# Transfers of 125 partitions as 112 and 13, and two first layer norms from one set of statistics

## The reference, cut to what matters

```
xn = LN(x)
x  = x + sage(xn, src, dst) + performer(LN(xn) * g1 + be1)   # kqv, exp features, gelu MLP
x  = x + attention(LN(x))                                    # router picks 1 of 3 weight sets, 8 heads, 1250 x 1250
xn = LN(x)
x  = x + gin(xn, adjacency) + slice_attention(xn)            # batch norms over the nodes
x  = x + moe(LN(x))    # 32 experts, each takes its top 39 of the 1250 tokens; 110 MB of weights
```

## Time and profile before

| | us |
|---|---|
| three runs | 1966.99, 1969.98, 1966.98 (median 1966.99) |
| profiled execution, whole | 1966.68 |
| its span in the trace | 1964.9 |

### The profile page before, as it was taken

The page is one execution under the profiler, slowest core; times in us unless marked ns, Lnnn a source line. Parts: engine busy times, 40 slices in busy tenths (PEclk is TensorE's granted clock), DMA queues, the critical chain, the costliest instruction groups (busy, mean ns, idle before and its releaser), DMA issues.

```text
span 1964.9 us, 19619 instructions
## 1 busy us (share of the span) xinstructions
PE 1617.7 (82%) x7674; PEld 1101.6 (56%) x7674; DVE 806.2 (41%) x1517; ACT 507.0 (26%) x734; POOL 391.3 (20%) x248
## 2 busy tenths in 40 slices
PE   1999969799998759888888886899889651999895
PEld 1546644366556548677777763555766541655452
DVE  5021160699204642577777755250344324111100
ACT  1210011021201132577777741100223110101000
POOL 3100030200301120344444424100220002222112
PEclk9999989899998879899999998999999855999997
DMA  4000100100110011100000012000200452799993
GB/s 171 0 0 1 41 4 0 59 1 1 82 46 1 6 65 66 27 14 14 14 14 14 22 37 120 0 22 0 86 1 0 206 206 95 285 403 400 408 418 126
DMA packets 23236, 170.74 MB, mean 87 GB/s; under 512 B 4259, under 2 KB 4805, under 8 KB 16886
## 3 DMA queue, kind: packets, MB, share of 16 engines
q1 hardware_dynamic: 19568, 164.44, 21.2%
q0 software_dynamic: 3584, 5.12, 1.2%
HBM read 153.06 MB, written 16.49 MB: 86 GB/s over the span
## 4 chain that ended last, share of the span: by engine, by line
PE 57%; DMA 16%; DVE 13%; ACT 6%; issue 5%; POOL 2%; another core or an unknown queue 1%; SPq 0%; DVEq 0%; POOLq 0%; ACTq 0%
PE psum L839 16%; DMA out_x<-arena,idx 12%; PE psum L849 9%; PE psum L866 6%; PE psum L978 6%; PE psum L1063 5%; PE psum L858 4%; PE psum L1051 3%; DVE arena_r L1458 3%; PE psum L1033 3%; DMA xf_dram<-arena 2%; DVE neg_max L1437 2%; ACT arena_r L762 1%; DVE ln_st L1217 1%; DVE arena L1225 1%
## 5 line engine op out<-in xcount | busy, mean ns | idle before, releaser
L839 PE MATMUL psum<-arena 125*128 125x512 f32 (+3 forms) x864 | 308.0, 518 | 14.2 <-DMA arena<-in_w_in 11.4
L839 PEld LDWEIGHTS psum<-arena 125*128 125x128 f32 (+1 forms) x864 | 164.5, 191 | 157.1 <-issue 143.3
L866 PE MATMUL psum<-arena 128*125 128x512 f32 (+3 forms) x464 | 163.0, 510 | 20.6 <-DVE arena L1565 9.0
L542 POOL TENSOR_SCALAR arena<-arena,row_inv 125x1250 f32<-125x1250 f32 x40 | 138.5, 3462 | 192.3 <-DVE row_inv L1445 192.3
L1198 PE MATMUL psum<-arena 128*39 128x512 f32 (+1 forms) x704 | 159.2, 609 | 13.0 <-DMA arena<-in_w_down 10.2
L1051 PE MATMUL psum<-ident,arena 125*125 125x125 f32 x800 | 125.8, 283 | 49.7 <-DVE arena_r L1458 48.4
L1458 DVE TENSOR_TENSOR arena_r<-psum,arena_r 125x500 fp32r<-125x500 f32 x200 | 131.9, 673 | 42.2 <-ACT arena_r L762 29.2
L1051 PEld LDWEIGHTS psum<-ident,arena 125*125 125x125 f32 x800 | 102.8, 188 | 63.0 <-DVE arena_r L1458 58.2
L762 ACT ACTIVATE arena_r<-psum 125x500 fp32r<-125x500 f32 x200 | 114.5, 587 | 87.9 <-PE psum L1051 87.8
L866 PEld LDWEIGHTS psum<-arena 128*125 128x125 f32 (+2 forms) x464 | 81.2, 191 | 99.1 <-issue 71.0
L978 PE MATMUL psum<-arena 125*125 125x512 bf16 (+1 forms) x588 | 120.1, 358 | 13.0 <-DVE arena L1349 11.5
(11 more groups left out here) (283 smaller groups left out, 2019.1 us busy)
## 6 DMA issues: line engine op xcount, KB each, us to landing
arena<-in_w_down SPq DMA_DIRECT2D x32, 2816.0 KB, 22.6
arena<-in_w_up SPq DMA_DIRECT2D x32, 682.5 KB, 19.7
a_spill<-arena SPq DMA_DIRECT2D x1, 6103.5 KB
arena<-a_spill SPq DMA_DIRECT2D x1, 6103.5 KB
bc<-k_dram SPq DMA_DIRECT2D x16, 312.5 KB, 4.3
gw<-in_gw SPq DMA_DIRECT2D x2, 2048.0 KB, 10.7
arena<-in_wkqv SPq DMA_DIRECT2D x1, 3072.0 KB, 16.5
arena<-in_x SPq DMA_DIRECT2D x10, 250.0 KB
```

Of the source, the lines that this page charges most:

```text
L542: pool.tensor_scalar(PR[i], PR[i], row_inv[:, i:i + 1], None, ALU.mult).then_inc(p_even, 1)
L839: ins = pe.matmul(o[0:w, lo:hi], lhs(c, m), rhs(c)[:, lo:hi], start=c == 0, stop=c == k - 1)
L866: ins = pe.matmul(o[0:p, 0:w], lhs(c, t), rhs(c, t), start=c == 0, stop=c == k - 1)
```

## The change

Every large transfer with X, XF or the adjacency on 125 partitions is made as two, of partitions 0 to 111 and 112 to 124 (`ROW_PARTS`), and what waits for it waits for 32 where it waited for 16. The x loads become three (one to a group) on SP with 112 partitions and three on ACT's queue with 13; `vec` moves to ACT's queue behind them, and `wkqv` ahead of the edge lists. The broadcast biases, also 125 partitions, stay as they are. Statistics are taken of x alone; the norm `mix1` comes first and straight from X, interleaved by group, and `xn` follows from the same statistics with a second column of powers, `xn_rs`.

```diff
+ROW_PARTS = (slice(0, 112), slice(112, TOK))
...
-LN_OUT = {n: TILES * i for i, n in enumerate(("xn", "mix1", "mix2", "ffn", "l1", "moe"))}
+LN_OUT = {n: TILES * i for i, n in enumerate(("mix1", "xn", "mix2", "ffn", "l1", "moe"))}
...
+            def store_rows(done, dst, src):
+                for rows_of in ROW_PARTS:
+                    sp.dma_start(dst[rows_of], src[rows_of]).then_inc(done, 16)
+
             x_v = a["x"].rearrange("(t p) d -> p t d", p=TOK)
-            for t in range(TILES):
-                load(f"x{t}", X[:, t], x_v[:, t])
-            load("vec", vec[:], a["vec"])
+            for g, (lo, hi) in enumerate(GROUPS):
+                load(f"x{g}", X[ROW_PARTS[0], lo:hi], x_v[ROW_PARTS[0], lo:hi])
+            load("wkqv", WKQV, a["wkqv"].rearrange("p (k n) -> p k n", k=C))
             load("edge_rows", edge_rows_i, a["dst_rows"])
             load("edges", edge_i[:, 0:EDGE_TILES], a["src_cols"])
             load("edges", edge_i[:, EDGE_TILES:2 * EDGE_TILES], a["dst_cols"])
-            load("wkqv", WKQV, a["wkqv"].rearrange("p (k n) -> p k n", k=C))
...
-            sp.dma_start(a_spill, part(6, 0, TILES * N, TOK)).then_inc(spilled, 16)
+            store_rows(spilled, a_spill, part(6, 0, TILES * N, TOK))
...
-            load("adj", part(6, 0, TILES * N, TOK), a_spill)
+            store_rows(loads["adj"], part(6, 0, TILES * N, TOK), a_spill)
...
-            sp.dma_start(out.rearrange("(t p) d -> p t d", p=TOK), X).then_inc(base_stored, 16)
+            store_rows(base_stored, out.rearrange("(t p) d -> p t d", p=TOK), X)
             sp.wait_ge(ln_out, LN_OUT["moe"] + TILES)
-            sp.dma_start(xf_dram.rearrange("(t p) d -> p t d", p=TOK), XF).then_inc(xf_stored, 16)
+            store_rows(xf_stored, xf_dram.rearrange("(t p) d -> p t d", p=TOK), XF)
...
-            for g in range(3):
-                rstd("xn", g)
+            for g, (lo, hi) in enumerate(GROUPS):
+                pool.wait_ge(ln_mv, LN_TILES["mix1", g])
+                pool.tensor_scalar(ln_rs[:, lo:hi], ln_mv_t[:, lo:hi, 1], 1.0 + LN_EPS, LN_EPS * LN_EPS,
+                                   ALU.mult, ALU.add).then_inc(ln_eps, 1)
+                pool.wait_ge(ln_eps, LN_NUMBER["mix1", g] + 1)
+                pool.tensor_tensor(ln_rs[:, lo:hi], ln_rs[:, lo:hi], minus_half[:, lo:hi], ALU.pow).then_inc(ln_rstd, 1)
+            done(pool.tensor_scalar(xn_rs[:], ln_mv_t[:, :, 1], LN_EPS, None, ALU.add))
+            pool.tensor_tensor(xn_rs[:], xn_rs[:], minus_half[:], ALU.pow).then_inc(xn_rstd, 1)
...
-            for g in range(3):
-                rstd("mix1", g)
-
             pool.wait_ge(loads["b2"], 16)
-            pool.wait_ge(ln_out, TILES)
+            pool.wait_ge(ln_out, 2 * TILES)
...
+            x_v = a["x"].rearrange("(t p) d -> p t d", p=TOK)
+            for g, (lo, hi) in enumerate(GROUPS):
+                act.dma_start(X[ROW_PARTS[1], lo:hi], x_v[ROW_PARTS[1], lo:hi]).then_inc(loads[f"x{g}"], 16)
+            act.dma_start(vec[:], a["vec"]).then_inc(loads["vec"], 16)
...
             for g in range(3):
-                stats("xn", g, X, lambda t: dve.wait_ge(loads[f"x{t}"], 16))
-            for g in range(3):
-                normalise("xn", g, X, XN)
-
-            for g in range(3):
-                stats("mix1", g, XN, lambda t: dve.wait_ge(ln_out, LN_OUT["xn"] + t + 1))
-            for g in range(3):
-                normalise("mix1", g, XN, XH1)
+                stats("mix1", g, X, lambda t: dve.wait_ge(loads[f"x{g}"], 32))
+                if g:
+                    normalise("mix1", g - 1, X, XH1)
+            normalise("mix1", 2, X, XH1)
+            dve.wait_ge(xn_rstd, 1)
+            for t in range(TILES):
+                dve.tensor_scalar(XN[:, t], X[:, t], ln_mv_t[:, t, 0:1], xn_rs[:, t:t + 1],
+                                  ALU.subtract, ALU.mult).then_inc(ln_out, 1)
```

More of the change, by code:

```diff
@@ L82 @@
 ADJ_COL = {x: COL["adj"] + n for n, x in enumerate(ADJ_ORDER)}
-LN_ORDER = [(n, g) for n in ("xn", "mix1", "mix2") for g in range(3)]
+LN_ORDER = [(n, g) for n in ("mix1", "mix2") for g in range(3)]
 LN_ORDER += [(n, g) for g in range(3) for n in ("sage", "ffn")]
@@ L128, in build @@
         ln_rs = sb("ln_rs", [TOK, TILES])
+        xn_rs = sb("xn_rs", [TOK, TILES])
         src_f = sb("src_f", [EDGE_TILE, EDGE_TILES])
@@ L286, in build @@
         ln_stats, ln_mv, ln_eps, ln_rstd, ln_out = [sem(n) for n in ("ln_stats", "ln_mv", "ln_eps", "ln_rstd", "ln_out")]
+        xn_rstd = sem("xn_rstd")
         dve_step, pool_step = sem("dve_step"), sem("pool_step")
@@ L318, in build @@
         loads = {n: sem("ld_" + n) for n in (
[1 row of a table removed]
+            "x0", "x1", "x2",
             "vec", "edges", "edge_rows", "wkqv", "wpt", "wo", "wm1", "wm2", "bv", "bo", "b2", "ws", "wn",
@@ L377, in _ @@
             sp.wait_ge(sel_ready, 1)
-            sp.wait_ge(spilled, 16)
+            sp.wait_ge(spilled, 32)
             sel = sp.value_load(sel_i[0:1, 0:1], min_val=0, max_val=2)
@@ L442, in _ @@
             sp.wait_ge(rows_free, ROW["gin_t"] + TILES)
-            sp.dma_start(out.rearrange("(t p) d -> p t d", p=TOK), X).then_inc(base_stored, 16)
+            store_rows(base_stored, out.rearrange("(t p) d -> p t d", p=TOK), X)
             sp.wait_ge(ln_out, LN_OUT["moe"] + TILES)
-            sp.dma_start(xf_dram.rearrange("(t p) d -> p t d", p=TOK), XF).then_inc(xf_stored, 16)
-            sp.wait_ge(base_stored, 16)
-            sp.wait_ge(xf_stored, 16)
+            store_rows(xf_stored, xf_dram.rearrange("(t p) d -> p t d", p=TOK), XF)
+            sp.wait_ge(base_stored, 32)
+            sp.wait_ge(xf_stored, 32)
             sp.wait_ge(rows_full, ROW["moe_t"] + 12)
@@ L602, in gather @@
                         in_offset=bass.IndirectOffsetOnAxis(ap=idx[:, e:e + 1], axis=0)).then_inc(gathered[b], 16)
-            pool.wait_ge(xf_stored, 16)
-            pool.wait_ge(base_stored, 16)
+            pool.wait_ge(xf_stored, 32)
+            pool.wait_ge(base_stored, 32)
             pool.wait_ge(rows_free, ROW["topk_t"] + 1)
@@ L695, in _ @@
             drain_cols("agg0", 4, lambda m: AGGT[:, m])
-            act.wait_ge(spilled, 16)
+            act.wait_ge(spilled, 32)
             act.wait_ge(loads["wn"], 16)
@@ L1482, in _ @@
             normalise("l1", 2, X, XN2)
-            dve.wait_ge(loads["adj"], 16)
+            dve.wait_ge(loads["adj"], 32)
             dve.wait_ge(loads["eps"], 16)
@@ L1594, in _ @@
             dve.wait_ge(rows_free, ROW["gate_t"] + 3)
-            dve.wait_ge(xf_stored, 16)
+            dve.wait_ge(xf_stored, 32)
             cur, other = SMT, SMT2
```

## The result

The changed kernel took 1913.27 us (median of 4, 1912.83 to 1914.17), the kernel before 1966.99 (median of 4, 1966.48 to 1969.98): ratio 0.9724, 95% interval 0.9708 to 0.9741. The forecast was 1906.9, with 1898 to 1915 as its range. The profiled execution took 1914.17 us, 7.3 above the forecast, with 1.9 of it around the span. What follows is where the 52.6 us between the two spans came from, and where the missing 7.3 went.

A forecast was written before the change was run, and what follows sets the result against it. PE is busy 82% of the span, so only stretches where PE stands still, waiting on slow 125-partition transfers, can be won: 25.9 + 10.9 + 23.0 = 59.8 us off 1966.7 gives 1906.9, range 1898 to 1915.

The forecast's parts named there:

- The reload: Adjacency load ahead of x_mid: at 420 GB/s PE no longer waits for `win`, 10.9 us won; any rate above 175 suffices.
- The stores: Two late stores ahead of the top-k: at 420 GB/s they land at about 1600, before the gate ends, 23.0 us won.
- The step's condition, 293 GB/s for the stores: The late stores' full win holds down to 5.12 MB in the 17.5 us before 1604, 293 GB/s.
- The spill at nothing: Store of the adjacency: over by 562 at the old rate, ACT's work behind it starts at 596.84, so splitting saves nothing.
- The start: x loads and first norm: PE starts at 13.2 and not at 39.10, 25.9 us won; ends of the term 15 and 27.
- 2.4 us at 420 GB/s: x loads: a group of four tiles, 1.02 MB, takes 2.4 us at 420 GB/s; group 1 there at 7.9.
- 112 partitions don't get the full rate: Rival on the split transfers: at 300 GB/s PE starts 2 us later, 1909; at 250 about 1913; chance 0.08.
- One engine for the 13 rows: Rival on the 13-partition pieces: one engine at 25.6 GB/s moves each, total win 38 us, 1929; chance 0.05.
- No more engines for 112: Rival on the split transfers: 112 partitions get no more engines, only 15.2 us at the start remain, 1952; chance 0.03.
- Slower by a low clock through k and q: Rival on k and q: at 1.2 GHz they take 67 us more, 7 us lost on the whole, 1974; chance 0.01.
- The added power over ten columns: POOL's power for XN: taken as 1.8 us, between 1.05 and 2.6; XN done at about 24, cover 20 us, no cost.
- the signs that I had named: Signs for the forecast: early PE and k, DMA over 350 GB/s, no waits at x_mid or top-k, 337 us from there.

The follow-up runs named there:

- x_by_partition_112: The changed kernel with x laid out by partition in DRAM, 20 KB in one piece each, loads still of 112 and 13 partitions: 1912.26 us.

## Why the prediction was right, and where it was off

**Right in kind, and in two of three terms.** The reload: 10.9 forecast, 11.1 measured between ffn_o and x_mid, 11.2 in the run that undid it. DMA moved 236 to 294 GB/s there and not 420, and it didn't matter, as the step had said for all rates above 175. The stores: 23.0 forecast, 22.1 measured between gin_t and the first MAX8, 22.5 by the run that undid it. The step's condition, 293 GB/s for the stores, was the tight one: the trace has them landing 0.9 us behind the gate. (By the step's own figures the stores started at 1587.1 and not at 1586.5, which makes the condition 303 GB/s.) The spill at nothing is shown by the run that undid it.

**The start was over-sized by 4.0 us**: 25.9 forecast, 21.9 measured. The term that failed is "2.4 us at 420 GB/s" for a group. I took the rate of a 128-partition row for 112 as the nearest one, with 128 GB/s as the other end. Group 1 landed at 12.3 and not at 7.9. The rest of the step held: from there on four statistics, the aggregates and four tiles took 4.7 us to PE's start, for 4.8 forecast; PE started 3.8 us late, and 0.2 were added on the way to k. The rival "112 partitions don't get the full rate" was the true case; it had a chance of 0.08. It was priced at 300 GB/s, 2 us, and the sum at 250 would have been nearer 4. Its total at 250 GB/s, 1913, is the time measured, and that is in part luck: it has the stores 2.4 us behind the gate (5.12 MB from 1586.5, less the gate's 1604.6), where 0.9 were measured, and nothing of the 2.5 us below that lie where nothing was changed. The forecast itself was 6.4 us off, and it is the range's allowance for the clock and the lower rate that holds the result. The count of 16 engines for 112 fitted; for the 13 the runs show only that it is more than one. What the counts leave out is that 16 engines needn't give 16 times the rate of one.

**The rest.** 7.3 us were missing in the profiled run. 4.0 are the start's, 0.9 the stores', less 0.2 for the reload. 2.5 lie where nothing was changed: k to ffn_o 0.1, x_mid to gin_t 0.9, the first up projection 1.1, the rest to the end 0.4 (286.0 for 285.6); the last 0.1 is outside the span. For the 1.1 and the 0.9 PE's clock is at hand: it restarts x_mid at the low level (0.50, 1.2 GHz) in both kernels; in the changed one the mean was 0.57 from 1194 to 1196, the fourth and fifth us of x_mid, where before it was already 0.62 over the first four. Over the first up projection the granted clock was 0.83 for 0.89, and PE was busy 15.8 us for 14.7, all of the 1.1. Such dips scatter from run to run, so I forecast their size as a range, and that is all that the runs allow. The longest up projection of the table isn't the clock alone: in x_by_partition_112 it took 21.6 us at 0.79, with PE busy for 18.1 of them, and what it waited for is open.

**The rivals.** One engine for the 13 rows: fell, 4.5 us measured for what would take 12.2. No more engines for 112: fell. Slower by a low clock through k and q: fell, they began 22 us earlier and took 67.40 us as before, at a granted clock of 1.00 (29 to 96 us). The added power over ten columns took 2.16 us on POOL (forecast 1.8, between 1.05 and 2.6), and XN was done at 28.1 us, not 24, ahead of the first sum of squares at 48.66: the cover of 20 us was there. Of the signs that I had named, three didn't come, all by the same slower load: PE's first transposes at 12 to 15 us (16.99), k at 24 to 27 (29.00), and DMA over 350 GB/s in the first 9 us (237 to 284 from 4 us on). The others came: x_mid 0.1 us behind ACT's last drain, the first MAX8 0.9 us behind the last copy, and 338.7 us from there to the end for 337. One sign of being wrong came as well: the top-k was still released by the store, though only by that 0.9 us.

**What the prediction didn't see.** It took the wait of the top-k for given and asked only how to shorten what was waited for. The run on the kernel before shows that 19 of the 22 us were to be had by moving that wait, with no transfer changed.

## What to carry to other kernels

Look at DMA's share beside its GB/s: here a third of the share with work queued meant that few engines took part, and a split of 125 partitions into 112 and 13 cured it; a full share at 250 GB/s meant that all took part and each was slow, and only a transfer of all 128 partitions cured that. A multiple of 16 isn't enough by itself: 96 partitions took as long as 112, with less to move. Before a waited-for transfer is made faster, read what the waiting engine does next: if its first 23 us don't touch the data, the wait belongs behind them. And a part priced at nothing because it is hidden is worth one run with that part undone.

## What the hardware showed unexpected

Fewer partitions aren't cheaper in a load: 112, 96, 80, 64 and 48 partitions, of 2.29 down to 0.98 MB, all took between 9.1 and 10.8 us, and 128 with 2.62 MB took 8.8. By the map of ports above all of them have 8 partitions on their fullest port. A store of 112 lost less (8.91 for 7.55 us). And 120 partitions, 14.5 us, are worse than 112, 10.7, though they seem the more natural cut.
